# A new order of steps in the first two groups of a fused attention and mixture-of-experts kernel: gated blocks in front of high parts, products in front of low parts and sums, a low part in front of an outer product

## The chip, the cores and the metric
One core of one Trainium2 chip. The metric is the device time of the whole kernel in microseconds (us), the median of several executions; lower is better. The engines are TensorE (PE in the profile: matrix products; PEld is its weight load), VectorE (DVE), ScalarE (ACT), GpSimd (POOL) and SyncE (SP), which here only issues DMAs. Each engine works through its own list of instructions in the order in which they are written; between engines the kernel waits on semaphores that it sets by hand.

## What is computed
The input x is [8, 256, 512]. The first half is a long convolution with outer products of heads, the second a mixture of experts:

```python
def _L0_xattn_ref(v, k, bias, x1, x2, num_heads):       # v = layernorm(x), x1 = x2 = ctx
    vr, x1r, x2r = (t.reshape(B, H, num_heads, L) for t in (v, x1, x2))
    kv = vr[:, :, :, None, :] * x2r[:, :, None, :, :]
    y = irfft(rfft(kv, n=2 * L) * rfft(k, n=2 * L)[None, :, None, None, :])[..., :L]
    y = y + kv * skip
    return jnp.einsum('bhijl,bhil->bhjl', y, x1r).reshape(B, D, L)
...
scores = sigmoid(xf @ gate_w.T)
topk_w, topk_idx = top_k(scores, 2)                      # weights normed to sum 1, times 2.5
shared_out = silu(xf @ shared_wg.T) * (xf @ shared_wu.T) @ shared_wd.T
h = silu(einsum('td,efd->etf', xf, exp_wg)) * einsum('td,efd->etf', xf, exp_wu)
all_out = einsum('etf,edf->etd', h, exp_wd)              # 8 experts, two picked for each token
...
x = x + _L0_xattn_ref(layernorm(x), k, bias, ctx, ctx, 8)
x = x + ffn(layernorm(x))
```

There are 32 head groups (H) of 8 heads, 2048 tokens, 8 experts of width 352, and shared experts of width 704.

## The kernel before, in words
The work has two stages. In the first, the 32 head groups s = 0 to 31 are taken in order, in four groups g of eight (s = 8g + h; HG = 8, G = 4). In the second, 39 tiles of 128 routed rows go through their expert. The shared experts of group g - 1 are computed in between the head groups of group g.

One head group s passes through these steps, and the change and the prediction's steps touch all of them:
- `outer(s)` (L654, instructions of L664, GpSimd): four products of 512 columns, v times context, into one of two buffers kv. It waits for the low part of s - 2, whose buffer it takes over, and outer(8g) also for the turned tiles of group g (L753). `second_outer` is the first one of this kind.
- `high_parts(s)` (L1122, instruction L1126, ScalarE): the half-precision high part of kv, into one of three buffers. It waits for outer(s).
- `low_parts(s)`: what is left of kv. For the s in the list DVE_LOWS (0, 1, 3, 5, 6, 7, 8, 9, 11 and every even s from 14 on) it runs on VectorE as one instruction (L1451, L1454), for the others on GpSimd as four (L687, L692).
- `turn_filter(s)` (L1115, L1119, ScalarE): the filter of s is brought into its form. SP loads the next filter after it (L433).
- `convolve(s)` (L826, TensorE): 30 matrix products of 512 columns through `split_products` (L821 to L823), in four blocks of 3, 6, 9 and 12, each block into its own bank. Block n waits for the low part and for product n of s - 1, which reads the bank that it writes.
- `products(s, h, g, blocks)` (L1462, L1468, VectorE): four products of a bank with the context, and `total(s, h)` (L1473, L1475), the sum over them. `finish` is both.

Between these lie, for a group g: `mix_out` (transposes of the mixed result, L843), which `mixed_tile` (L1648, L1652) reads and adds to x, two banks in turn, so that the third transpose waits for the first mixed tile; `mixed_moments`, the inverse root on GpSimd (L697), `mixed_shift` (L1490), `feed_norm` on ScalarE (L1170) and `feed_low` on VectorE (L1520), after which SP turns the rows (L480) for the gate and the shared experts. A gated block (g, m), m = 0 to 5, is a `gate_up` on TensorE (24 products, 12 for m = 0), which waits for the gated product of block m - 1 (L893); `gated_silu` on ScalarE (L1201), `gated_product` on VectorE (L1624, L1631), `gated_high` on ScalarE (L1208, L1215) and `gated_low` on VectorE (L1634, L1639). The skip term of the attention goes through `skip_product` (L1503, L1510, VectorE), `skip_sum` (L853, L857, TensorE) and `skip_term` (L1513, L1517 and L1518, VectorE); its buffers hm and silu are those of the gated blocks. `values(g)` is a layer norm, `prepare` its transposes and `turned` (L1160, L1166, ScalarE) the copy of these from the banks. `shared(i)` (L1239, L1242 and L1244, ScalarE) and `piece(i)` (L720, L723, GpSimd) split nine pieces of the shared weights into high and low parts. `pick` and `pairs` choose the experts and the rows, and `send_rows` (GpSimd) scatters the rows.

No planner sets the order: each engine's list is written out by hand, in loops over g and h with exceptions, as in ScalarE's list:

```python
for h in range(1, HG + 1):
    ...
    elif 0 < g < G - 1 and h == 6:
        turn_filter(s0 + h + 1)
        turned(g + 1, range(2, Q))
        high_parts(s0 + h + 2)
        gated(g - 1, h - 3)
        continue
```

TensorE's own order (L950 to L1027) and SP's (L488 to L570) are the same before and after.

## Time and profile before

| what | value |
| --- | --- |
| median of 3 runs | 709.83 us (709.59 to 712.0) |
| time of the profiled execution | 713.41 us |
| its span | 711.4 us |
| granted clock of TensorE over the span | 0.976 |
| busy share: TensorE, VectorE, GpSimd, ScalarE | 92%, 63%, 50%, 41% |
| first stage, up to the last convolution of group 3 | to about 398 us |
| first routed tile to the end | from about 478 us |

The span is the time from the first to the last instruction of the profiled execution; its own time is 2.0 us longer, and it is itself 3.6 us longer than the median. A TensorE clock of 1.00 is 2.4 GHz, and 0.5 is 1.2 GHz. Busy shares are means over stages with different limits.

### The profile page before, as it was taken

What the parts mean: (1) busy time and instruction counts of PE and PEld (TensorE: products, weight loads), DVE (VectorE), ACT (ScalarE), POOL (GpSimd) and SP (SyncE); (2) the same over time, 40 slices, a digit from 0 to 9 for tenths busy, and PEclk for the clock granted to TensorE, in tenths of its full rate; (3) what the DMA queues carried; (4) which work ended last, traced back from release to release, by engine and by line L of the source; (5) the groups of instructions that cost most, each with busy time, mean ns of one, the idle gap of its engine ahead of it and who ended that gap; (6) DMA issues with size and microseconds to landing.
All of it is one profiled execution on the core that took longest, in us unless ns stands there. A gap on an engine that the chain in (4) does not pass through costs nothing.

```text
span 711.4 us, 11546 instructions
## 1 busy us (share of the span) xinstructions
PE 655.6 (92%) x3475; PEld 331.4 (47%) x3476; DVE 447.1 (63%) x723; ACT 293.9 (41%) x374; POOL 354.6 (50%) x294
## 2 busy tenths in 40 slices
PE   5979878977999999899999999889979999999994
PEld 3534333433444444344444434345545555555552
DVE  4999988786987695998796778864431221112210
ACT  4356568434233653223541278343432233323321
POOL 2999899925686454695566005600132222332223
PEclk8899999999999999999999999999999999999998
DMA  6944326012234810224313668958998888788864
GB/s 196 289 118 111 98 89 147 17 43 53 102 116 86 182 30 16 90 76 56 94 30 120 249 188 283 384 130 171 237 162 122 126 129 130 129 138 128 132 93 60
DMA packets 130519, 91.57 MB, mean 129 GB/s; under 512 B 96992, under 2 KB 110816, under 8 KB 129952
## 3 DMA queue, kind: packets, MB, share of 16 engines
q1 hardware_dynamic: 121728, 71.49, 41.1%
q0 software_dynamic: 8176, 18.75, 14.5%
q10 hardware_dynamic: 576, 0.82, 0.5%
q8 instruction: 23, 0.38, 0.2%
q14 instruction: 16, 0.13, 0.1%
HBM read 46.32 MB, written 25.65 MB: 101 GB/s over the span
## 4 chain that ended last, share of the span: by engine, by line
PE 55%; DVE 17%; POOL 9%; SPq 5%; ACT 5%; issue 5%; DMA 3%; POOLq 0%; DVEq 0%; ACTq 0%
PE banks L821 16%; PE banks L823 15%; PE banks L822 15%; POOL arena L664 6%; PE banks L913 2%; DVE mixT L1475 2%; DVE arena L1468 2%; PE banks L917 2%; PE banks L918 2%; SPq L583 2%; DVE stats L1481 2%; POOL arena L723 1%; DVE silu L1510 1%; DMA arena<-split_filters 1%; DMA x_tok<-in_x 1%
## 5 line engine op out<-in xcount | busy, mean ns | idle before, releaser
L664 POOL TENSOR_TENSOR arena<-arena 128x512 f32<-128x512 f32 x120 | 141.9, 1214 | 58.7 <-ACT arena L1166 31.5
L783 POOL DMA_INDIRECT out<-xf,ids x39 | 61.7, 1583 | 183.8 <-DMA out<-xf,ids 96.4
L821 PE MATMUL banks<-arena 128*128 128x512 f16 (+1 forms) x330 | 125.0, 379 | 15.8 <-DVE arena L1468 12.1
L822 PE MATMUL banks<-arena 128*128 128x512 f16 (+1 forms) x330 | 124.8, 378 | 0.0
L823 PE MATMUL banks<-arena 128*128 128x512 f16 (+1 forms) x330 | 124.6, 378 | 0.0
L821 PE MATMUL banks<-arena,normed 128*128 x312 | 98.2, 315 | 4.0 <-DVE hm L1853 4.0
L823 PE MATMUL banks<-arena,normed 128*128 x312 | 98.3, 315 | 0.0
L822 PE MATMUL banks<-arena,normed 128*128 x312 | 98.2, 315 | 0.0
L1851 DVE SCALAR_TENSOR_TENSOR hm<-banks,silu 128x256 f32<-128x256 f32 x39 | 16.6, 425 | 121.5 <-PE banks L823 102.5
L1126 ACT ACTIVATE arena<-arena 128x2048 f16<-128x2048 f32 x31 | 59.0, 1904 | 70.6 <-POOL arena L664 68.0
L1468 DVE TENSOR_TENSOR arena<-banks,arena 128x512 f32<-128x512 f32 x128 | 80.5, 681 | 12.2 <-PE banks L823 11.9
L1475 DVE TENSOR_REDUCE mixT<-arena 128x256 f32<-128x2048 f32 x32 | 73.1, 2285 | 1.0
L821 PE MATMUL banks<-xf,arena 128*128 128x512 f16 x176 | 67.0, 380 | 2.6 <-DVE hm L1631 2.6
L692 POOL TENSOR_TENSOR arena<-arena 128x512 f16<-128x512 f32 x56 | 64.0, 1173 | 6.5 <-ACT arena L1126 6.5
L822 PE MATMUL banks<-xf,arena 128*128 128x512 f16 x176 | 66.8, 380 | 0.0
L823 PE MATMUL banks<-xf,arena 128*128 128x512 f16 x176 | 66.7, 379 | 0.0
L821 PEld LDWEIGHTS banks<-arena 128*128 128x128 f16 x330 | 32.7, 99 | 58.2 <-issue 17.3
L1119 ACT ACTIVATE arena<-arena 128x1024 f16<-128x1024 f16 x31 | 32.6, 1052 | 54.0 <-PE banks L823 41.5
L823 PEld LDWEIGHTS banks<-arena 128*128 128x128 f16 x330 | 32.8, 100 | 37.9 <-issue 1.4
L1360 ACT CAST x_tok<-hm 128x384 f16<-128x384 f32 x37 | 18.9, 511 | 73.8 <-DVE hm L1853 71.8
L822 PEld LDWEIGHTS banks<-arena 128*128 128x128 f16 x330 | 32.8, 99 | 35.5 <-issue 1.7
L821 PE MATMUL banks<-arena,mixT 128*128 x117 | 44.4, 379 | 1.2 <-issue 1.2
(196 smaller groups left out, 1082.0 us busy)
## 6 DMA issues: line engine op xcount, KB each, us to landing
arena<-split_filters SPq DMA_DIRECT2D x31, 256.0 KB, 3.7
arena<-in_expert_w SPq DMA_DIRECT2D x12, 544.0 KB, 8.0
stages<-in_expert_w SPq DMA_DIRECT2D x10, 544.0 KB, 4.7
arena<-in_ctx_hidden SPq DMA_DIRECT2D x4, 1024.0 KB, 8.1
arena<-in_ctx SPq DMA_DIRECT2D x8, 512.0 KB, 6.2
out<-x_tok SPq DMA_DIRECT2D x6, 512.0 KB, 5.5
x_tok<-in_expert_w SPq DMA_DIRECT2D x5, 544.0 KB
mixT<-in_expert_w SPq DMA_DIRECT2D x5, 544.0 KB
```

Source lines behind the costliest of these rows:

```text
L664: nc.gpsimd.tensor_tensor(kv[s % 2][:, lb * COLS:(lb + 1) * COLS].rearrange("p (b j i) -> p b j i", i=NH, j=NH), v[:, a, None, :].to_broad ...
L692: nc.gpsimd.tensor_tensor(kvl[s % SPLITS][:, c], kv[s % 2][:, c], kvh[s % SPLITS][:, c], ALU.subtract).then_inc(kvl_by_pool, 1)
L783: nc.gpsimd.indirect_dma_start(out=out, out_offset=bass.IndirectOffsetOnAxis(ap=ids[slot][:, 0:1], axis=0), in_=yg[slot], in_offset=None, ...
L821: nc.tensor.matmul(dst, wh, xh, start=(k == 0), stop=False)
L822: nc.tensor.matmul(dst, wh, xl, start=False, stop=False)
L823: last = nc.tensor.matmul(dst, wl, xh, start=False, stop=(k == n - 1))
L1119: nc.scalar.activation(filt[s % 2].rearrange("p (t l) -> p t l", t=2), backward(filt_raw, 2), ACT.Copy).then_inc(filt_ready, 1)
L1126: nc.scalar.activation(kvh[s % SPLITS], kv[s % 2], ACT.Copy).then_inc(kvh_ready, 1)
L1360: nc.scalar.copy(by_token[slot][:, 0:FK * P], hm[:, 0:FK * P]).then_inc(r_hh, 1)
L1468: nc.vector.tensor_tensor(prod[:, n * COLS:(n + 1) * COLS].rearrange("p (b j i) -> p b j i", i=NH, j=NH), bank[n].rearrange("p (b j i) -> ...
L1475: nc.vector.tensor_reduce(heads(mixT)[:, :, h * NH:(h + 1) * NH], prod.rearrange("p (a j i) -> p a j i", i=NH, j=NH), AX_X, ALU.add).then_ ...
L1851: nc.vector.scalar_tensor_tensor(out=hm[:, 0:whole], in0=up[:, 0:whole], scalar=1 / WS, in1=silu[:, 0:whole], op0=ALU.mult, op1=ALU.mult)
```

## The change
Only orders of steps are changed, on ScalarE, GpSimd and VectorE; `split_products`, the steps themselves and the orders of TensorE and SP are not. By engine:
- GpSimd: in group 1 the low part of h = 7 is issued before the outer product of s = 16 instead of behind it, and shared piece 8 one head group later.
- ScalarE: in group 0 shared piece 3 moves in front of high part 7, so that turned tiles 2 and 3 follow right behind that part; in group 1 shared piece 7 stands in front of filter 11, gated blocks 0, 1, 3 and 5 in front of the high parts beside them; in group 2 the silu and the high copy of gated blocks 2 and 3 are moved in the same way.
- VectorE: in group 0 the moments and low part 3 stand in front of total 1, two or three products in front of low parts 7 and 8; at the start of group 1 three products stand in front of low part 9, total 8 between the third and the fourth mixed tile, and single products and low parts 10 to 12 are interleaved with the feed's low parts; in group 2 the products of s = 19 stand in front of `pick`; in group 3 total 24 stands in front of the fourth mixed tile.

```diff
@@ GpSimd
-            pieces_at = {..., (1, 3): [7], (1, 4): [8]}
+            pieces_at = {..., (1, 3): [7], (1, 5): [8]}
                 for h in range(HG):
-                    low_parts(s0 + h)
+                    if g != 1 or h != HG - 1:
+                        low_parts(s0 + h)
+                    if g == 1 and h == HG - 2:
+                        low_parts(s0 + h + 1)
@@ ScalarE
-            shared_at = {(0, 3): [0], ..., (0, 6): [3], (0, 7): [4], (0, 8): [5], (1, 1): [6], (1, 2): [7, 8]}
+            shared_at = {(0, 3): [0], ..., (0, 7): [4], (0, 8): [5], (1, 1): [6]}
                     if g == 1 and h == 2:
+                        shared(7)
                         next_parts(s0 + h + 1)
+                        shared(8)
+                        load_sigmoid(0)
+                        continue
...
+                    if g == 0 and h == 5:
+                        turned(1, range(0, 2))
+                        turn_filter(h + 1)
+                        shared(3)
+                        high_parts(h + 2)
                         continue
+                    if g == 0 and h == 6:
+                        turned(1, range(2, Q))
+                    elif g == 1 and h == 3:
+                        scores(0)
+                        load_silu(0)
+                        gated(0, 0)
+                        next_parts(s0 + h + 1)
+                        continue
+                    elif g == 1 and h in (4, HG):
                         turn_filter(s0 + h + 1)
+                        gated(0, h - 3)
                         high_parts(s0 + h + 2)
                         continue
+                    elif g == 1 and h == 5:
+                        next_parts(s0 + h + 1)
+                        values(2)
+                        gated(0, 2)
+                        turned(2, range(0, 2))
+                        continue
+                    elif g == 1 and h == 6:
                         turn_filter(s0 + h + 1)
+                        turned(2, range(2, Q))
+                        gated(0, 3)
                         high_parts(s0 + h + 2)
+                        continue
+                    elif g == 2 and h == 5:
+                        turn_filter(s0 + h + 1)
+                        gated_silu(1, 2)
+                        high_parts(s0 + h + 2)
+                        gated_high(1, 2)
+                        turned(3, range(0, 2))
+                        continue
+                    elif g == 2 and h == 6:
+                        turned(3, range(2, Q))
+                        gated_silu(1, 3)
+                        turn_filter(s0 + h + 1)
+                        gated_high(1, 3)
+                        high_parts(s0 + h + 2)
                         continue
@@ VectorE, group 0
             for h in range(1, HG):
-                low_parts(h + 1)
-                finish(h, h, 0)
                 if h == 1:
+                    products(h, h, 0)
                     value_moments(1)
+                    low_parts(3)
+                    total(h, h)
+                    continue
+                if h == 2:
+                    products(h, h, 0)
                     values(1)
+                    total(h, h)
+                elif h >= HG - 2:
+                    products(h, h, 0, range(0, h - HG + 4))
+                    low_parts(h + 1)
+                    products(h, h, 0, range(h - HG + 4, LB))
+                    total(h, h)
+                else:
+                    low_parts(h + 1)
+                    finish(h, h, 0)
@@ VectorE, groups 1 to 3
+                if g == 1:
+                    products(s0, 0, g, range(0, LB - 1))
+                    low_parts(s0 + 1)
+                    products(s0, 0, g, range(LB - 1, LB))
+                    mixed_tile(0, 0)
+                    mixed_tile(0, 1)
+                    mixed_tile(0, 2)
+                    dve.wait_ge(outT_ready, Q * g)
+                    total(s0, 0)
+                    mixed_tile(0, 3)
+                    mixed_moments(0)
+                    mixed_moments(0, True)
+                    products(s0 + 1, 1, g, range(0, 1))
+                elif g == 2:
...
+                else:
+                    low_parts(s0 + 1)
+                    products(s0, 0, g)
+                    mixed_tile(g - 1, 0)
+                    mixed_tile(g - 1, 1)
+                    mixed_moments(g - 1)
+                    mixed_tile(g - 1, 2)
+                    dve.wait_ge(outT_ready, Q * g)
+                    total(s0, 0)
+                    add_shared(g - 2, 0)
+                    mixed_tile(g - 1, 3)
+                    add_shared(g - 2, 1)
+                    mixed_moments(g - 1, True)
                 mixed_shift(g - 1)
                 low_parts(s0 + 2)
...
                 if g == 1:
-                    products(s0 + 1, 1, g)
-                    feed_low(0, range(0, 2))
+                    products(s0 + 1, 1, g, range(1, LB))
+                    feed_low(0, range(0, 1))
                     total(s0 + 1, 1)
-                    feed_low(0, range(2, Q))
+                    feed_low(0, range(1, 3))
+                    products(s0 + 2, 2, g, range(0, 1))
+                    low_parts(s0 + 3)
+                    feed_low(0, range(3, Q))
+                    products(s0 + 2, 2, g, range(1, LB))
+                    total(s0 + 2, 2)
...
                 gated(g - 1, 0)
                 if g == 1:
+                    products(s0 + 3, 3, g, range(LB - 1, LB))
+                    total(s0 + 3, 3)
                     skip_product(1, 0)
                     skip_product(1, 1)
-                    products(s0 + 3, 3, g, range(LB - 1, LB))
-                    total(s0 + 3, 3)
...
+                elif g == 2:
+                    finish(s0 + 3, 3, g)
+                    pick(g - 1)
+                    value_moments(g + 1)
+                    values(g + 1)
+                    gated(g - 1, 1)
```

## Rows read from the trace of the kernel before

**Rows 1.** The page: busy time by engine, and three groups of instructions

```profile
PE 655.6 (92%) x3475; PEld 331.4 (47%) x3476; DVE 447.1 (63%) x723; ACT 293.9 (41%) x374; POOL 354.6 (50%) x294
...
L1468 DVE TENSOR_TENSOR arena<-banks,arena 128x512 f32<-128x512 f32 x128 | 80.5, 681 | 12.2 <-PE banks L823 11.9
L1475 DVE TENSOR_REDUCE mixT<-arena 128x256 f32<-128x2048 f32 x32 | 73.1, 2285 | 1.0
```

**Rows 2.** Windows: stretch, its length, busy by engine, TensorE's clock, DMA share, GB/s

```profile
480.00:700.00 220.00, 214.75 (x1272) 124.92 (x1270) 56.03 (x127) 70.43 (x123) 57.86 (x37) 0.99 0.84 138
```

**Rows 3.** Who TensorE waited for: us in total, times, longest

```profile
PE banks L821 <- DVE arena L1468: 12.1, 7, 3.1
PE banks L857 <- DVE hm L1510: 5.9, 3, 4.5
```

**Rows 4.** Timeline of TensorE: start, us, instruction, count, wait in front and its releaser

```profile
85.97 0.38 PE L821 MATMUL banks<-arena 128*128 128x512 f16 x1 [1.57 <-DVE arena L1468]
96.62 1.70 PE L843 MATMUL banks<-con,mixT 128*128 128x128 f32 x8 [3.15 <-DVE x_tok L1652]
...
116.23 0.38 PE L821 MATMUL banks<-arena 128*128 128x512 f16 x1 [3.06 <-DVE arena L1468]
...
150.14 0.38 PE L821 MATMUL banks<-arena 128*128 128x512 f16 x1 [1.52 <-DVE arena L1468]
160.20 0.39 PE L821 MATMUL banks<-xf,arena 128*128 128x512 f16 x1 [2.56 <-DVE hm L1631]
...
177.99 1.24 PE L857 MATMUL banks<-hm,con 128*128 128x512 f32 x2 [4.49 <-DVE hm L1510]
...
254.42 0.38 PE L821 MATMUL banks<-arena 128*128 128x512 f16 x1 [1.60 <-DVE arena L1468]
...
302.11 1.10 PE L857 MATMUL banks<-hm,con 128*128 128x512 f32 x2 [1.10 <-DVE hm L1510]
```

**Rows 5.** Windows around waits of TensorE; the clock is the third number from the right

```profile
47.00:55.00 8.00, 6.63 (x30) 2.87 (x30) 7.90 (x11) 3.37 (x4) 8.00 (x8) 1.00 0.11 33
...
97.00:101.00 4.00, 4.00 (x16) 2.15 (x15) 3.90 (x7) 3.48 (x3) 4.00 (x4) 0.59 0.65 255
...
116.00:122.00 6.00, 5.77 (x26) 2.38 (x27) 5.45 (x8) 5.49 (x7) 6.00 (x6) 0.72 0.70 176
...
178.00:182.00 4.00, 3.56 (x6) 1.10 (x7) 3.86 (x10) 0.70 (x1) 3.26 (x3) 0.60 0.10 32
```

**Rows 6.** Timeline of VectorE, ScalarE and GpSimd, 65 to 90 us

```profile
67.40 2.58 DVE L1454 TENSOR_TENSOR arena<-arena 128x2048 f16<-128x2048 f32 x1
...
74.62 2.28 DVE L1454 TENSOR_TENSOR arena<-arena 128x2048 f16<-128x2048 f32 x1
...
75.69 1.05 ACT L1166 COPY arena<-banks 128x512 f32<-128x512 f32 x2
...
65.74 6.20 POOL L664 TENSOR_TENSOR arena<-arena 128x512 f32<-128x512 f32 x4
...
76.81 4.14 POOL L664 TENSOR_TENSOR arena<-arena 128x512 f32<-128x512 f32 x4 [2.79 <-ACT arena L1166]
...
83.00 6.22 POOL L664 TENSOR_TENSOR arena<-arena 128x512 f32<-128x512 f32 x4
```

**Rows 7.** Timeline of GpSimd and ScalarE, 97 to 112 us

```profile
104.61 4.50 POOL L692 TENSOR_TENSOR arena<-arena 128x512 f16<-128x512 f32 x4
...
103.70 1.91 ACT L1126 ACTIVATE arena<-arena 128x2048 f16<-128x2048 f32 x1 [1.44 <-POOL arena L664]
```

**Rows 8.** Timeline of ScalarE and VectorE around 172 us

```profile
171.40 1.91 ACT L1126 ACTIVATE arena<-arena 128x2048 f16<-128x2048 f32 x1 [4.24 <-POOL arena L664]
...
173.83 0.69 DVE L1631 SCALAR_TENSOR_TENSOR hm<-banks,silu 128x512 f32<-128x512 f32 x1 [5.39 <-ACT silu L1206]
```

**Rows 9.** Timeline of VectorE and ScalarE in group 2

```profile
253.58 2.48 DVE L1468 TENSOR_TENSOR arena<-banks,arena 128x512 f32<-128x512 f32 x4
...
279.95 1.91 ACT L1126 ACTIVATE arena<-arena 128x2048 f16<-128x2048 f32 x1 [4.25 <-POOL arena L664]
```

37 lines of the change are left out of this document (9 added, 28 removed).

## The prediction
> **What bounds the kernel.** I read five views. The page comes first: TensorE is busy 92% of the span, no other engine over 63% [rows 1]. The windows come second: from 480 us to the end TensorE is busy 214.75 of 220 us at a clock of 0.99 [rows 2], so the routed tiles leave next to nothing, and what comes earlier in time shifts them as a block. Third, who TensorE waits for: 12.1 us for VectorE's products (L1468) in 7 waits and 5.9 us for its skip products (L1510) in 3 [rows 3]. Fourth, where these waits lie: all large ones stand between 84 and 180 us, in the end of group 0 and in group 1, and small ones at 254 and 302 us [rows 4]. Fifth, the clock: behind a wait of 3.06 to 4.49 us it is granted at 0.59 to 0.72 of full (2.4 GHz with stretches of 1.2 GHz), behind the one of 2.93 us in front of 47.6 us it is 1.00 [rows 5]. The three falls cost 41% of 4 us, 28% of 6 us and 40% of 4 us: 1.6 to 1.7 us each, on top of the waits.
>
> I write conv(s), outer(s), high(s), low(s), products(s) and total(s) for the steps of head group s (s = 8g + h), turn(s) for the filter. One conv is 6.5 us, one product 0.62 from start to start, a total 2.2, a low part 2.2 on VectorE and 4.5 on GpSimd, a high part 1.8, four outer products 4.13 when nothing disturbs them [rows 1, 6, 7].
>
> **The change, stage by stage.** No instruction is added or removed; a split products(s) keeps its four instructions. So each term is a start time of TensorE, before and after, worked out along the orders.
>
> *Group 0, h = 1 to 5.* Moments and low(3) go in front of total(1). VectorE has no idle time here and the sum of its work in front of products(2) is the same, so conv(3) and conv(4) keep their starts: 0. GpSimd gets the variance 2.2 us earlier but low(3) now falls in outer(4); I count it 1.3 us earlier, hidden.
>
> *Group 0, h = 6 and 7.* Here the change speaks against itself. Before, low(7) runs at 74.62, while GpSimd is idle: it waits until 76.81 for ScalarE's copy of the turned tiles at 75.69 [rows 6]. After, this copy stands before the shared piece and right behind high(7). That one waits for outer(7), which begins at about 64.5 (65.74 less the 1.3) and has low(6) inside: 64.5 + 4.13 + 2.1 = 70.8, high(7) to 72.7, the copy to 73.6. So outer(8) starts at 73.7, three microseconds earlier; but low(7) now stands behind two products, at 75.86, in the middle of outer(8). What such a meeting costs is shown: outer(9) took 6.22 us with low(8) inside, 2.1 more than alone, and low(6) took 2.58, held up 0.4 us by the outer product that had begun [rows 6]. So low(7) waits for one of outer(8)'s four instructions, 0 to 1.03 us; by the start times above it is 0.9 (next boundary 76.8). It ends at 79.0 and conv(7) starts at 79.1, not 77.75: **1.35 lost**. The same for low(8): in front of it three products, ready at 84.3 (total(6) ends at 82.45), held up until 85.2 by outer(9) (begun at 82.1, behind outer(8) to 80.0 and a shared piece of 2.1), done at 87.4: conv(8) at 87.5, not 85.97 [rows 4]: 1.5 lost in all. The Trainium skill (SBUF — State Buffer, "SBUF: two separate sides") calls the shared port pair of VectorE and GpSimd an exclusive lock that the first to start holds for its whole instruction; the trace agrees, and by this rule these two steps speak against the change.
>
> *Mixed tiles.* conv(8) ends at 94.0. VectorE by then has low(9) (92.5 to 94.8, held behind three products) and one product left, so the first mixed tile is read at 95.45, and TensorE's second pair of transposes starts at 96.25 (before 96.62 [rows 4]). The wait shrinks from 3.15 to 1.3 us because the transposes start later, and the clock should not fall. With total(8) out of the way of the fourth transpose conv(9) starts at 97.3 (98.12) and ends at 103.8, 1.9 us earlier, most of it the clock.
>
> *conv(10) and conv(11).* The moments end at 103.5 behind total(8), so GpSimd's low(10) starts at 104.6, as before [rows 7], and conv(10) at 105.8 waits for its first block, and once more for its second: end 112.8 (113.0). low(11), behind one product of 10, is ready at 112.4, held up 0.8 us by outer(12), done 115.4; turn(11) now stands behind a shared piece and ends at 115.6 (ScalarE's row norm ends at 112.7). conv(11) starts at 115.7 (116.23). So the 3.06 us wait stays, as 2.9 us: it has two causes now. Whether the clock falls behind it the trace does not say: bounds 0 and 1.7 us; nearest is the row of 2.93 us without a fall, so I take 0. End of the first three blocks 119.95 (121.8).
>
> *To conv(13).* Logits, gated block 0, gate_up(0,1), two skip sums: conv(12) starts at 133.4 (135.1). The gated block no longer waits for high(13); product(11,3) is done before the skip products. VectorE goes through skip products, terms, gated(0,1), pick and moments and reaches products(12) at 146.2, where it was at 149.3: conv(13) at 146.9 (150.14 [rows 4]).
>
> *gate_up(0,3).* values(2) end at 153.9, silu 154.4, product 155.15: it starts at 155.2 (160.20), the wait is 1.0 us instead of 2.56. conv(14) at 161.9.
>
> *The large one.* Before, ScalarE does high(16) in front of gated(0,3); high(16) waits until 171.40 for outer(16), VectorE idles 5.39 us for the silu, and TensorE then waits 4.49 us for the skip products behind it [rows 8, 4]. After, gated(0,3) comes at 162.1. VectorE's order decides: products(13) and total(13) end at 163.4, product(0,3) 164.1, copy 164.7, low 165.4, skip products to 168.4, while conv(14) ends at 168.4. Wait gone, and with it 0.43 us for the rank and the fall of the clock (1.6): conv(15) at 175.3, before 187.06, **11.8 earlier**. GpSimd: low(15) now goes into its idle time in front of outer(16) (about 149 to 154), needed at 175; shared piece 8 ends at 149.3, and the copy that waits for it is at 155.2. Queued behind the new waits of ScalarE is high(14), at 136.9 instead of 133.7, needed by VectorE at 156.5. SP: turning the rows comes 3 us later (last low part at 116.0) and filter 12 behind it, landed at about 121, used at 126: hidden. Skip sum (2,2) will wait 0.5 us for gated(0,4). conv(16) at 189.2, before 200.5: **11.3 earlier**.
>
> *Group 2.* products(19) stood behind pick and moments, at 253.58 [rows 9], and cost 1.60 us [rows 4]. After they run first, but pick, moments, inverse root and shift then stand in front of gated(1,1), done at about 260.3 on the old clock, and gate_up(1,2) waits for it: 1.3 of the 1.6 are given back. gated(1,3) no longer waits for high(24), which was released at 279.95 [rows 9]: the waits 0.31, 0.58 and 1.10 in front of the skip sums go. Sum **2.3**.
>
> *Group 3.* Shift 1.6 us later, logits have some 8 us in hand: 0.
>
> **Sum:** 11.3 + 2.3 = 13.6 us. The profiled execution took 713.41 (span 711.4), so 699.8; the median of the three runs shown is 3.58 lower, 709.83, which gives 696.2. I say **696.5**.
>
> **Rivals.** Half a per cent, 3.5 us, is about what a measurement of this kernel can tell from no change.
> *A, the large wait stays* (17%). VectorE reaches gated(0,3) late, or another wait (the rank, the turned tiles) takes its place. For: by my times its skip products end just when conv(14) ends, with no slack. Against: the wait for the silu was 5.39 us. Loss 4.49 + 1.6 of clock, partly: 701.5.
> *B, falls of the clock and held-up low parts in group 1* (10%). conv(10) and conv(11) both wait over 2 us; two falls of 1.7 and two more holds of 1.03 on low(9) and low(11), and a longer wait for mixed tiles, 2 us: 704.
> *C, no change* (4%). The freed time comes back as waits for the experts' weights, whose transfers begin behind group 3. Against: they are all started by events that move with TensorE, and TensorE does not wait there [rows 2]. 709.8.
> *D, slower* (4%): the lock on the port. If ScalarE's copy does not come earlier, low(7) still locks outer(8); GpSimd, which has no idle time from 76.8 to 119 us, is 2.1 us late in every later step, and TensorE's waits for products turn into waits for low parts. With conv(7) 1.35 and conv(8) another 1.5 us late, and nothing won behind them, it ends at 709.8 + 2.1 + 2.9 = 714.8. It decides only when GpSimd is late by more than the slack of low(13), which I find done at 138.1 and used at 146.9, 8.8 us. It is the same rule of the lock; the rule alone, taken as the whole effect, would give this time.
> The forecast keeps 65%.
>
> **Range.** With no hold of low(7) and low(8) the chain reaches conv(16) 13.6 instead of 11.3 us earlier (-2.3), and if group 2 gives back nothing, -1.3; to the small waits behind 404 us I leave 2: 690.5 at the low end. Upward the clock (+1.7), the holds, A and B: 704.5. Outside lie C, D and a part of B, with some doubt in so long a chain. Below 706.3 (faster by over 0.5%) lie the forecast, A and nearly all of B: 91%; within 0.5%: 5%; slower: 4%.
>
> **What would show it.** Right: no wait of TensorE near 175 us before the first skip sum of group 2 and VectorE's silu wait of 5.39 us gone; conv(16) about 11 us earlier; low(7) longer than 2.3 us or outer(8) about 6.2 us; conv(7) later than 77.75; a wait of about 2.9 us still in front of conv(11); a new wait below 1.3 us in front of gate_up(1,2). Wrong: any wait over 2 us between 120 and 190 us; a clock below 0.9 behind conv(11); a routed stage that takes more than before from its first tile to its end.

## The result, and the profile of the changed kernel

| | before | after |
| --- | --- | --- |
| median | 711.33 us (709.05 to 714.25, 12 runs) | 705.5 us (701.37 to 709.77, 12 runs) |
| profiled execution, its span | 713.41 us, 711.4 us | 709.77 us, 707.7 us |
| granted clock over the span | 0.976 | 0.974 |
| conv(8), conv(16), conv(31), each after the start of conv(1) | 57.17, 171.72, 362.33 | 61.61, 168.28, 358.56 |
| from conv(31) to the end of the span | 320.3 | 320.3 |

The ratio of after to before is 0.9924, 95% interval 0.9895 to 0.9952: faster by 5.8 us, where I had forecast 13.6, and outside my range. The direction was right, the size was not. A few executions of low15_undone, of h6_low15 and of before beside them were far slower at a lower clock (770 to 1332 us); every median, number of runs and ratio below is of the others. Starts in the tables are read in the timeline of TensorE and counted from conv(1) of the same execution; the rows shown have the time from the start of the span.

The page of after, its busy times and the groups that answer to [rows 1] (VectorE's products are now L1500, its totals L1507, its low parts L1486; TensorE's lines are three higher):

```profile
PE 656.8 (93%) x3475; PEld 332.2 (47%) x3476; DVE 454.9 (64%) x723; ACT 294.3 (42%) x374; POOL 346.2 (49%) x294
...
L1500 DVE TENSOR_TENSOR arena<-banks,arena 128x512 f32<-128x512 f32 x128 | 80.7, 680 | 10.6 <-PE banks L826 10.2
L1486 DVE TENSOR_TENSOR arena<-arena 128x2048 f16<-128x2048 f32 x17 | 46.4, 2728 | 0.0
```

The low parts in before (groups by line):

```profile
L1454 DVE TENSOR_TENSOR arena<-arena 128x2048 f16<-128x2048 f32 x17 | 40.5, 2382 | 2.6 <-ACT arena L1126 2.6
```

VectorE has the same 723 instructions and is busy 7.8 us more. The products cost what they did; the 17 low parts cost 5.9 us more, with a mean of 2.73 us instead of 2.38, and a low part that nothing disturbs takes 2.28 [rows 6]. That is the first place to look.

The timeline of TensorE in after, the rows with a wait (start, us, instruction, wait in front and its releaser), against [rows 4]:

```profile
48.59 0.38 PE L824 MATMUL banks<-arena 128*128 128x512 f16 x1 [3.85 <-DVE arena L1500]
...
82.03 0.38 PE L824 MATMUL banks<-arena 128*128 128x512 f16 x1 [1.65 <-issue]
90.48 0.38 PE L824 MATMUL banks<-arena 128*128 128x512 f16 x1 [1.82 <-issue]
...
100.25 1.85 PE L846 MATMUL banks<-con,mixT 128*128 128x128 f32 x8 [2.25 <-DVE x_tok L1684]
...
120.00 0.39 PE L824 MATMUL banks<-arena 128*128 128x512 f16 x1 [2.48 <-ACT arena L1122]
...
137.96 1.10 PE L860 MATMUL banks<-hm,con 128*128 128x512 f32 x2 [0.65 <-DVE hm L1542]
139.53 1.10 PE L860 MATMUL banks<-silu,con 128*128 128x512 f32 x2 [0.47 <-DVE silu L1542]
161.76 0.39 PE L824 MATMUL banks<-xf,arena 128*128 128x512 f16 x1 [0.42 <-DVE hm L1663]
...
190.18 1.10 PE L860 MATMUL banks<-hm,con 128*128 128x512 f32 x2 [1.65 <-DVE hm L1542]
...
258.18 0.39 PE L824 MATMUL banks<-xf,arena 128*128 128x512 f16 x1 [2.04 <-DVE hm L1663]
...
298.40 1.10 PE L860 MATMUL banks<-hm,con 128*128 128x512 f32 x2 [1.50 <-DVE hm L1542]
```

The wait of 4.49 us near 178 is gone, as forecast. What was not forecast: waits all through group 0, and 2.04 and 1.50 us in group 2. Windows around the new waits (the clock is the third number from the right):

```profile
101.00:105.00 4.00, 4.00 (x17) 2.09 (x16) 3.56 (x4) 1.85 (x1) 2.12 (x3) 0.65 0.24 54
...
120.00:124.00 4.00, 4.00 (x12) 1.57 (x13) 3.93 (x5) 3.97 (x4) 4.00 (x3) 0.61 0.65 144
```

So two of the three falls of [rows 5] are still there, behind waits of 2.25 and 2.48 us, shorter than the 2.93 us in front of 47.6 behind which before had a clock of 1.00. I had taken all three as gone. One is there that before did not have: behind the 3.85 us in front of 48.6 the stretch from 47 to 55 us has 0.79, where before had 1.00 [rows 5].

Which of these waits has a fall behind it is not fixed by the kernel. low15_undone (below) has the same orders as after up to this point and the same wait in front of conv(11), and its clock stays at 1.00 (a row of the timeline and a window):

```profile
119.38 0.39 PE L821 MATMUL banks<-arena 128*128 128x512 f16 x1 [2.48 <-ACT arena L1119]
120.00:124.00 4.00, 4.00 (x45) 2.17 (x44) 3.93 (x5) 3.98 (x4) 4.00 (x4) 1.00 0.81 200
```

And gates_only (below) has before's orders in group 0 and the same wait of 2.93 us in front of conv(3), and its clock falls, where before's did not:

```profile
47.73 0.38 PE L824 MATMUL banks<-arena 128*128 128x512 f16 x1 [2.93 <-DVE arena L1496]
47.00:55.00 8.00, 7.28 (x26) 3.00 (x27) 7.90 (x11) 3.37 (x4) 8.00 (x8) 0.79 0.11 33
```

The same holds of two more waits: 2.25 us at the mixed tiles (0.57 over 100 to 104 us in after, 1.00 in h6_undone) and 2.54 us in front of conv(10) (1.00 over 105 to 109 us in moments_first, 0.62 in moments_g2v); in each pair the kernels have the same orders up to there. So each profile holds falls that another execution of the same kernel may not have.

The starts, counted from conv(1), and the stretch in which the change lies, for all kernels of this study:

| kernel | conv(8) | conv(12) | conv(15) | conv(16) | conv(31) | conv(8) to (16) | conv(31) to end |
| --- | --- | --- | --- | --- | --- | --- | --- |
| before | 57.17 | 106.28 | 158.26 | 171.72 | 362.33 | 114.55 | 320.3 |
| after | 61.61 | 111.59 | 153.02 | 168.28 | 358.56 | 106.67 | 320.3 |
| g0_only | 61.62 | 106.64 | 160.95 | 174.32 | 365.09 | 112.70 | 315.5 |
| g0_undone | 57.14 | 104.09 | 148.18 | 163.44 | 354.59 | 106.30 | 319.2 |
| h1_undone | 57.78 | 104.26 | 148.34 | 163.60 | 354.26 | 105.82 | 314.4 |
| moments_first | 57.91 | 106.54 | 148.00 | 163.26 | 353.39 | 105.35 | 316.3 |
| piece_split | 57.66 | 104.75 | 148.92 | 164.18 | 355.99 | 106.52 | 314.8 |
| h6_only | 57.17 | 104.61 | 153.22 | 171.47 | 362.98 | 114.30 | 316.9 |
| gates_only | 57.15 | 107.03 | 148.46 | 163.72 | 355.54 | 106.57 | 320.0 |
| h6_undone | 61.62 | 110.95 | 157.66 | 171.03 | 360.91 | 109.41 | 317.7 |
| low15_undone | 61.63 | 108.08 | 153.68 | 171.94 | 360.62 | 110.31 | 320.2 |
| h6_low15 | 57.15 | 106.28 | 153.22 | 168.47 | 358.80 | 111.32 | 316.2 |
| start_undone | 58.10 | 105.60 | 148.66 | 163.92 | 353.47 | 105.82 | 316.7 |
| g2_undone | 61.63 | 111.52 | 152.98 | 168.23 | 359.47 | 106.60 | 317.3 |
| h1_g2v_undone | 57.74 | 104.20 | 148.28 | 163.53 | 353.93 | 105.79 | 319.2 |
| moments_g2v | 57.91 | 103.50 | 147.57 | 162.82 | 353.00 | 104.91 | 317.4 |
| split_best | 58.09 | 106.14 | 150.30 | 165.56 | 354.94 | 107.47 | 317.0 |

The last column scatters by 6 us between kernels that differ in nothing there (more on it at the end). The column conv(31) is the finer instrument, and the medians stand beside it. How fine it is shows in kernels that are the same up to some point: moments_first and moments_g2v, the same up to conv(16), are 3.04 us apart at conv(12), where the clock fell behind conv(11)'s wait in one and not in the other, and still 0.44 at conv(16); after and low15_undone, the same up to there, are 3.51 apart at conv(12). From conv(16) to conv(31) the six kernels with after's order of group 2 and uncut pieces take between 188.7 and 191.2 us. A difference of 1 us at conv(31), or of 3 at conv(12), is not a finding by itself.

### The profile page after: what moved, and what is told of

The parts are those of the page before. It is cut to its first block, busy times and chain, and to the rows that moved or that the text cites. A ratio compares the mean times of both kernels' runs of the same rounds, so it can differ in the third digit from the quotient of the medians.

```text
span 707.7 us, 11553 instructions
## 1 busy us (share of the span) xinstructions
PE 656.8 (93%) x3475; PEld 332.2 (47%) x3476; DVE 454.9 (64%) x723; ACT 294.3 (42%) x374; POOL 346.2 (49%) x294
## 4 chain that ended last, share of the span: by engine, by line
PE 53%; DVE 26%; issue 6%; SPq 5%; ACT 5%; DMA 3%; POOLq 0%; POOL 0%; DVEq 0%; ACTq 0%
PE banks L824 15%; PE banks L825 15%; PE banks L826 15%; DVE arena L1500 5%; DVE mixT L1507 4%; DVE arena L1486 3%; PE banks L916 2%; DVE stats L1513 2%; PE banks L921 2%; PE banks L920 2%; SPq L583 1%; DVE silu L1542 1%; PE banks L846 1%; DMA arena<-split_filters 1%; DVE hm L1663 1%
## 5 line engine op out<-in xcount | busy, mean ns | idle before, releaser
L664 POOL TENSOR_TENSOR arena<-arena 128x512 f32<-128x512 f32 x120 | 134.0, 1148 | 51.3 <-DVE arena L1486 31.6
L1500 DVE TENSOR_TENSOR arena<-banks,arena 128x512 f32<-128x512 f32 x128 | 80.7, 680 | 10.6 <-PE banks L826 10.2
L1507 DVE TENSOR_REDUCE mixT<-arena 128x256 f32<-128x2048 f32 x32 | 73.1, 2284 | 1.1 <-PE banks L846 0.2
L692 POOL TENSOR_TENSOR arena<-arena 128x512 f16<-128x512 f32 x56 | 65.8, 1203 | 6.5 <-ACT arena L1129 6.5
L1486 DVE TENSOR_TENSOR arena<-arena 128x2048 f16<-128x2048 f32 x17 | 46.4, 2728 | 0.0
```

The source lines that it names most:

```text
L664: nc.gpsimd.tensor_tensor(kv[s % 2][:, lb * COLS:(lb + 1) * COLS].rearrange("p (b j i) -> p b j i", i=NH, j=NH), v[:, a, None, :].to_broad ...
L692: nc.gpsimd.tensor_tensor(kvl[s % SPLITS][:, c], kv[s % 2][:, c], kvh[s % SPLITS][:, c], ALU.subtract).then_inc(kvl_by_pool, 1)
L1486: nc.vector.tensor_tensor(kvl[s % SPLITS], kv[s % 2], kvh[s % SPLITS], ALU.subtract).then_inc(kvl_by_dve, 1)
L1500: nc.vector.tensor_tensor(prod[:, n * COLS:(n + 1) * COLS].rearrange("p (b j i) -> p b j i", i=NH, j=NH), bank[n].rearrange("p (b j i) -> ...
L1507: nc.vector.tensor_reduce(heads(mixT)[:, :, h * NH:(h + 1) * NH], prod.rearrange("p (a j i) -> p a j i", i=NH, j=NH), AX_X, ALU.add).then_ ...
```

## Experiments on group 0

**g0_only**: the kernel before with the change's orders of group 0 alone.

```
             for h in range(1, HG):
-                low_parts(h + 1)
-                finish(h, h, 0)
...
+                if h == 1:
+                    products(h, h, 0)
+                    value_moments(1)
+                    low_parts(3)
+                    total(h, h)
+                    continue
...
```

> The kernel before with the new order of group 0 alone. Theory H: conv(8) starts at about 90.5 instead of 86, and the kernel is 3 to 4.5 us slower than before, about 715. Theory L: as before, 711.

Measured 711.64 us (12 runs), ratio 1.0001 (0.998 to 1.0022). conv(8) at 61.62, exactly after's 61.61 (before 57.17): group 0 alone loses 4.45 us there, and conv(31) comes 2.8 us later than in before. The median doesn't show it: it is 711.64, where before's own runs beside it had 711.44, as theory L had it and not theory H. The table shows where the 4.45 us go. At conv(12) 0.36 us of them is left: the wait in front of the mixed tiles is 0.93 us instead of 3.15 and no fall is behind it (1.00 over 97 to 101 us, before 0.59). The rest of the 2.8 us at conv(31) begins behind the wait of 2.56 us in front of gate_up(0,3), which before has too, but here with a fall of the clock (0.59 over 160 to 164 us, before 1.00). So in the kernel before, with its own long waits in group 1, the loss of group 0 is absorbed nearly whole.

**g0_undone**: the opposite, the kernel after with group 0 as before, on VectorE and on ScalarE.

```
-                        turn_filter(h + 1)
-                        shared(3)
-                        high_parts(h + 2)
+                        next_parts(h + 1)
...
+                low_parts(h + 1)
+                finish(h, h, 0)
...
```

> The changed kernel with all of group 0 put back to the old order (VectorE's head groups 1, 2, 6, 7 and ScalarE's shared piece 3). Theory H (VectorE's low parts are held up by GpSimd instructions that the new order of group 0 puts in front of them): conv(8) starts at 86, not 90.5, low parts 5 to 9 take 2.3 to 3.2 us each as before, and the whole is 4 to 5 us faster than the changed kernel, about 701. Theory L (group 0 costs nothing of note, the missing gain was never there in groups 1 and 2): within 1 us of the changed kernel, about 705.5.

Measured 701.95 us (6 runs), ratio 0.9867 (0.9827 to 0.9906); conv(8) 57.14, conv(31) 354.59, 4.0 us better than after. In the kernel after the loss of group 0 goes through to the end nearly whole; from conv(8) to conv(16) the two take 106.67 and 106.30 us. Why it is not absorbed here as in g0_only was not tried.

**h1_undone** and **moments_first** take the step of h = 1 apart. The first has total(1) in front of both the moments and low(3), as before; the second leaves the moments where the change put them and moves low(3) alone.

```
                 if h == 1:
-                    products(h, h, 0)
+                    finish(h, h, 0)
                     value_moments(1)
                     low_parts(3)
-                    total(h, h)
                     continue
```

```
                     value_moments(1)
-                    low_parts(3)
                     total(h, h)
+                    low_parts(3)
                     continue
```

> The changed kernel with only the step at h = 1 put back (total 1 in front of the moments and low part 3). Theory H in the form that this step starts it (GpSimd gets 1.3 us ahead, so that its shared pieces of 2.1 us stand in front of low parts 5 and 6): low(3) takes 2.3 instead of 3.2 us, low(5) and low(6) together 6 instead of 8.1 us, conv(6) starts at 71 instead of 73.7, and the kernel is 2 to 3 us faster than the changed one, about 703. If the later steps (products in front of low parts 7 and 8) are the cause: less than 1 us.

> The changed kernel with low part 3 behind total 1 again, but the moments still in front of both: of the step at h = 1 only the moments stay moved. If the moved low part (a hold of 1 us, and GpSimd released 1.3 us early) starts the loss: as with the whole step put back, low(3) 2.3 us, low(5) 3.2 us, conv(31) begins 353 to 354.5 us behind conv(1) instead of 358.6. If the early variance (the moments) is what puts GpSimd out of step: conv(31) stays at about 358.6 behind conv(1).

h1_undone 703.57 us (6 runs), ratio 0.9888 (0.9859 to 0.9918), conv(8) 57.78; moments_first 701.87 us (4 runs), ratio 0.9859 (0.9805 to 0.9913), conv(8) 57.91. Of the 4.44 us at conv(8) they get back 3.83 and 3.70. So it is not the moments, and the steps of h = 6 and 7, against which my prediction argued at length, are worth the remaining 0.6 to 0.7 us at most and not 1.5 (low(7), which I had held up, takes 2.28 us in h1_undone): it is low(3) in front of total(1). The timelines show how. The low parts on VectorE and GpSimd's instructions in after:

```profile
42.32 3.20 DVE L1486 TENSOR_TENSOR arena<-arena 128x2048 f16<-128x2048 f32 x1
60.27 4.27 DVE L1486 TENSOR_TENSOR arena<-arena 128x2048 f16<-128x2048 f32 x1
69.17 3.83 DVE L1486 TENSOR_TENSOR arena<-arena 128x2048 f16<-128x2048 f32 x1
...
60.26 2.13 POOL L723 TENSOR_TENSOR arena<-xf,arena 128x1024 f16<-128x1024 f32 x1
64.62 4.14 POOL L664 TENSOR_TENSOR arena<-arena 128x512 f32<-128x512 f32 x4 [2.23 <-DVE arena L1486]
68.71 2.13 POOL L723 TENSOR_TENSOR arena<-arena 128x1024 f16<-128x1024 f32 x1
```

and the same in moments_first:

```profile
59.83 3.20 DVE L1486 TENSOR_TENSOR arena<-arena 128x2048 f16<-128x2048 f32 x1
67.66 2.59 DVE L1486 TENSOR_TENSOR arena<-arena 128x2048 f16<-128x2048 f32 x1
...
56.75 4.14 POOL L664 TENSOR_TENSOR arena<-arena 128x512 f32<-128x512 f32 x4
60.85 4.18 POOL L723 TENSOR_TENSOR arena<-xf,arena 128x1024 f16<-128x1024 f32 x1
64.99 6.19 POOL L664 TENSOR_TENSOR arena<-arena 128x512 f32<-128x512 f32 x4
```

In after, GpSimd begins a shared piece, one instruction of 2.13 us, at 60.26; VectorE's low part begins at 60.27, ends at 64.54 and so takes 4.27 us instead of 2.28: it stood for the whole piece. GpSimd's next outer product then waits 2.23 us, until the low part is done, so that it comes behind it again, and so does the next piece. That order feeds itself: low parts 5 to 9 took 4.27, 3.83, 2.98, 3.10 and 3.73 us. It begins with low(3), which takes 3.20 us in front of total(1) and 2.28 behind it: counted from conv(1), low(5) starts at 31.40 instead of before's 30.76, and GpSimd's outer(5) at 17.50 instead of 18.90. This is not scatter: in g0_only, g2_undone, h6_undone and low15_undone, which have the same order of group 0, low parts 5 to 8 take the same within 0.01 us. In moments_first VectorE's low part falls into the outer products, whose single instructions are about 1.03 us, and takes 3.20 and 2.59; there it is GpSimd that stands (4.18 and 6.19 us instead of 2.13 and 4.14), and GpSimd had time. The Trainium skill (SBUF — State Buffer, "SBUF: two separate sides") has the port pair locked by the one that starts first, for a whole instruction; these rows agree for low parts, outer products and pieces: whoever comes second pays what is left of the other's instruction. Not every instruction of VectorE meets GpSimd: the 32 totals (L1507) take 2.27 to 2.29 us each in after, with GpSimd busy beside them or not.

**piece_split** tests this by the length of the instruction: the order of after, unchanged, with each shared piece cut in four on GpSimd.

```
-                nc.gpsimd.tensor_tensor(shared_piece(i, d_l, gu_l), as_piece(shared_raw(i), i),
-                                        shared_piece(i, d_h, gu_h), ALU.subtract).then_inc(shared_l, 1)
+                whole = (shared_piece(i, d_l, gu_l), as_piece(shared_raw(i), i), shared_piece(i, d_h, gu_h))
+                for k in range(4):
...
```

> The changed kernel with each shared piece on GpSimd as four instructions of a quarter each. Theory H: a low part waits for at most one of these, 0.55 us, in place of up to 2.1; low parts 5 to 9 take 2.2 to 2.9 us each, conv(8) starts 2 to 4 us earlier than at 90.5, the whole about 702 to 703. Rival (the low parts wait for GpSimd's whole run of work, not for one instruction, or GpSimd paces the chain): the low parts stay at 3 to 4.3 us and the time within 1 us of 705.5, or above it for the 27 added instructions.

Measured 702.75 us (6 runs), ratio 0.9882 (0.9846 to 0.9918), conv(8) 57.66. low(3) still takes 3.21 us, but low parts 5 to 9 take 2.81, 2.38, 2.28, 2.29 and 2.70, and of the 4.44 us of group 0 0.49 is left although every order is after's. Two doubts can be settled from the trace. The cut makes GpSimd 0.45 us late before low(5), which could have let low(5) go first; but it still begins 0.01 us behind GpSimd, at 60.88 behind 60.87, and takes 0.53 us more than alone, a quarter of 2.13. And the clock, which fell behind conv(3)'s wait in after, did not fall here (1.00 over 49 to 53 us); but VectorE begins products(3) 26.44 us behind conv(1) here and 26.42 in after, so that fall moved nothing on VectorE. With this the cause is shown from both sides: by the order and by the length of the instruction that stands in the way.

## Experiments on group 1

**h6_only** is the step of the large wait, alone on the kernel before. The prediction's 11.8 us at conv(15) are the sum of all steps up to there; 6.8 of them are this step's, from conv(14) to conv(15).

```
                         turned(g + 1, range(2, Q))
+                        if g == 1:
+                            gated(g - 1, h - 3)
                         high_parts(s0 + h + 2)
-                        gated(g - 1, h - 3)
+                        if g == 2:
+                            gated(g - 1, h - 3)
```

> The kernel before with one step moved: gated block (0, 3) in front of high part 16 on ScalarE. Theory G (this step is what the large gain in group 1 comes from): the wait of 4.49 us in front of the first skip sum of group 2 goes with its fall of the clock, conv(15) begins 5 to 6.7 us earlier, the kernel 5 us faster, 706. Rival (the gain needs VectorE to be ahead from the start of group 1): VectorE reaches the skip products late, the wait shrinks by under 2 us, 709.5.

Measured 711.0 us (10 runs), ratio 0.999 (0.9959 to 1.0021). conv(15) comes 5.0 us earlier, and conv(16) 0.25: all but nothing is left. The wait for the silu is gone and another one stands behind it. Theory G was right for conv(15) and wrong for the time, where it had 706.

**gates_only** is the kernel before with all moves of the gated blocks in group 1, with low(15) and piece 8 on GpSimd, product(11,3) on VectorE and the small step of group 3, and nothing in group 0, at the start of group 1 or in group 2.

```
+                    elif g == 1 and h == 3:
+                        scores(0)
+                        load_silu(0)
+                        gated(0, 0)
+                        next_parts(s0 + h + 1)
+                        continue
+                    elif g == 1 and h in (4, HG):
...
```

> The kernel before with one part of the change: in group 1 the gated blocks stand in front of the high parts on ScalarE (h = 3, 4, 5, 6 and 8), low(15) in front of outer(16) on GpSimd and product(11,3) with total(11) in front of the skip products. Group 0, the start of group 1 and group 2 are as before. Theory (VectorE paces group 1, and what the change wins is its idle time in front of the silu): conv(8) to conv(16) takes 114.55 us before and 106.67 after; of the 7.9 us the stretch from conv(12) on has 8.7 and the stretch up to it -0.9, so the gated blocks alone give all of it. conv(16) minus conv(1) 171.72 before, here 162.5 to 164.5, VectorE's idle time for the silu between conv(8) and conv(16) 3 to 5 us instead of 12.5, conv(31) minus conv(1) 353.5 to 355.5 (before 362.33), median 701 to 704. Rival (my prediction's steps: the start of group 1 carries part of it, because it decides when VectorE reaches the gated blocks): the gates alone give only 5 to 6 us, conv(31) minus conv(1) 356.5 to 357.5. Second rival (what gated(0,3) alone showed: what is won in one place is given back at the next, so without group 0's earlier turned tiles nothing is won): within 1 us of before, 361.5 to 363.

Measured 701.77 us (5 runs), ratio 0.9838 (0.9792 to 0.9883): the part is faster than the whole. conv(8) to conv(16) 106.57 us (before 114.55, after 106.67), VectorE's idle time for the silu there 4.5 us instead of 12.5. conv(31) at 355.54 is at the upper edge of the theory's interval. The gates with low(15) hold the whole gain of group 1.

**h6_undone** is after with gated(0,3) behind high(16) again.

```
                         turned(2, range(2, Q))
-                        gated(0, 3)
                         high_parts(s0 + h + 2)
+                        gated(0, 3)
                         continue
```

> The kernel after with gated(0,3) behind high(16) again, everything else of the change kept: the step to which my prediction gave 11.8 us. Theory (VectorE paces group 1; gated(0,3) in front of high(16) is what keeps VectorE from the idle time for the silu; alone it won nothing only because VectorE's later gated blocks waited): VectorE idles 3 to 6 us longer for the silu, TensorE waits over 3 us in front of skip_sum(2,0) again, conv(15) 4 to 6 us later than after's 153.02 behind conv(1), conv(16) 3 to 6 us later than 168.28 behind conv(1), conv(31) minus conv(1) 361.5 to 364.5, median 708 to 711. Rival (the same 0 here as when the step was made alone): conv(16) within 1 us, conv(31) minus conv(1) 358 to 359.5. Rival of my prediction's sum (the whole large wait with its fall of the clock): 11 us lost, conv(31) minus conv(1) 368 to 370.

Measured 707.57 us (11 runs), ratio 0.9932 (0.9902 to 0.9962). TensorE waits 3.44 us in front of skip_sum(2,0), VectorE idles 5.39 us for the silu, conv(15) is 4.6 us later than after's and conv(16) 2.75, conv(31) 2.35 (a little less than the theory had). The rival with 11 us had taken the prediction's sum up to conv(15) for the step. The step is worth 0 alone and 2.4 to 2.75 in company, so something in the company belongs to it. The timeline of VectorE in h6_only, a part of the sixteen instructions between rank and products(14), shows what:

```profile
177.28 1.03 DVE L1567 TENSOR_TENSOR wsum<-top 128x4 f32<-128x4 f32 x1
178.35 0.99 DVE L1571 TENSOR_SCALAR wsum<-wsum 128x4 f32<-128x4 f32 x1
...
180.40 0.99 DVE L1575 TENSOR_SCALAR stages<-wtop 128x4 f32<-128x4 f32 x1
```

the same instructions in gates_only:

```profile
174.00 0.15 DVE L1592 TENSOR_TENSOR wsum<-top 128x4 f32<-128x4 f32 x1
174.19 0.17 DVE L1596 TENSOR_SCALAR wsum<-wsum 128x4 f32<-128x4 f32 x1
...
174.81 0.17 DVE L1600 TENSOR_SCALAR stages<-wtop 128x4 f32<-128x4 f32 x1
```

and GpSimd, in h6_only:

```profile
171.74 5.39 POOL L692 TENSOR_TENSOR arena<-arena 128x512 f16<-128x512 f32 x4
177.22 4.15 POOL L664 TENSOR_TENSOR arena<-arena 128x512 f32<-128x512 f32 x4
```

Three instructions of four numbers a row take 1 us each where they took 0.15 to 0.17, and one of eight numbers 0.77 where it took 0.17: each stands behind one of GpSimd's instructions of 1.03 us. The other twelve of the sixteen hardly change. From the rank to the next products VectorE needs 7.83 us here, 3.88 in before (whose pairs begin 5 us later; GpSimd is through at 181.26, and only the first of them meet it) and 4.43 in gates_only and after, where low(15), L692, has been done long before, and GpSimd's last outer product ends just before wsum, the first row shown, begins: at 173.86 in gates_only (wsum at 174.00), at 178.38 in after (178.52). The gain of the early silu was paid back in these tiny instructions: 5.39 us of idle time less 3.95 more for the pairs. The next two kernels test this reading.

**low15_undone**: after with only GpSimd's low(15) back in its old place. **h6_low15**: before with h6_only's move and that of low(15).

```
-                    if g != 1 or h != HG - 1:
-                        low_parts(s0 + h)
-                    if g == 1 and h == HG - 2:
-                        low_parts(s0 + h + 1)
+                    low_parts(s0 + h)
```

> The kernel after with low(15) back in its old place on GpSimd, behind outer(16). Theory (in gated(0,3) alone, what the early silu won on VectorE, 5.39 us of idle time, was given back by the sixteen tiny instructions of the rank and the pairs: from the first of them to products of conv(15) they took 7.83 us where the kernel before took 3.88 and the gates alone 4.43, because each stood behind one instruction of about 1 us of low(15) or an outer product on GpSimd; the move of low(15) empties GpSimd in that stretch): here this stretch on VectorE takes 7 to 8 us instead of after's 4.43, conv(16) comes 2.5 to 5 us later than after's 168.28 behind conv(1), conv(31) minus conv(1) 361 to 363.5 (after 358.56), median 708 to 710.5. Rival (my prediction's view: low(15) only fills idle time of GpSimd, needed at 175, so its place is worth nothing): conv(16) within 0.5 us, conv(31) minus conv(1) 358 to 359.

> The kernel before with two moves: gated(0,3) in front of high(16) on ScalarE, and low(15) in front of outer(16) on GpSimd. gated(0,3) alone won nothing (conv(16) minus conv(1) 171.47, before 171.72). Theory (the two belong together: low(15) out of the way keeps the tiny instructions of the pairs short, and then VectorE reaches the skip products of group 2 in time): VectorE's stretch from the rank to the products of conv(15) 4 to 4.9 us instead of 7.83, the wait in front of skip_sum(2,2) under 1.5 us instead of 2.96 and no fall of the clock behind it, conv(16) minus conv(1) 165.5 to 168, conv(31) minus conv(1) 356.5 to 359, median 704.5 to 708. Rival (the pairs are not the cause: the other gated blocks that stand behind high parts, at h = 4 and 5, make VectorE late): conv(16) minus conv(1) over 169.5, conv(31) minus conv(1) 360 to 363.

low15_undone 710.56 us (8 runs), ratio 0.9989 (0.9957 to 1.002): without this one move, which I had put down as filling idle time, the time cannot be told from before's. The pairs take 7.83 us again and conv(16) comes 3.66 us later than after's, 3.0 of it between conv(15) and conv(16), where h6_only and h6_low15 differ by the same 3.0. Part of that comes back in group 2: conv(31) is 2.1 us later, less than the theory's 2.4 to 4.9, and still 1.7 us earlier than before's. The other 3 us of the median are not in the first stage. h6_low15 704.92 us (5 runs), ratio 0.9913 (0.988 to 0.9946): the pairs take 4.42 us, the wait in front of skip_sum(2,2) is 1.65 us instead of 2.96, and conv(16) is at 168.47 instead of 171.47 (the theory's interval ended at 168; this execution had a fall behind gate_up(0,3) that h6_only's had not, and its conv(14) is 2.2 us later than there). Row by row TensorE in h6_only and, behind it, in h6_low15:

```profile
192.08 1.10 PE L857 MATMUL banks<-hm,con 128*128 128x512 f32 x2 [2.96 <-DVE hm L1513]
193.01 1.62 PE L857 MATMUL banks<-silu,con 128*128 128x512 f32 x2
```

```profile
189.43 1.10 PE L860 MATMUL banks<-hm,con 128*128 128x512 f32 x2 [1.65 <-DVE hm L1516]
190.37 1.02 PE L860 MATMUL banks<-silu,con 128*128 128x512 f32 x2
```

The second row of each pair shows the clock as well: the same two products take 1.62 us behind the wait of 2.96 and 1.02 behind that of 1.65. h6 and low(15) are one step in two places. Together they are worth 3.25 of the 8.0 us at conv(16), in an execution with one fall more than before's; the other gated blocks are the rest.

**start_undone** is h1_g2v_undone (below) with the start of group 1 put back on VectorE: mixed tiles, moments, low parts for the logits.

```
                 if g == 1:
-                    products(s0, 0, g, range(0, LB - 1))
                     low_parts(s0 + 1)
-                    products(s0, 0, g, range(LB - 1, LB))
-                    mixed_tile(0, 0)
...
+                    products(s0, 0, g)
+                    mixed(g - 1)
...
```

> The kernel after with h = 1 of group 0 and VectorE's step of group 2 as before (the fastest so far), and with VectorE's order at the start of group 1 (mixed tiles, moments, copies of the logits' low parts, products(9) and (10)) put back too. Theory (VectorE's work at the start of group 1 counts as soon as group 0 is not late): conv(8) to conv(12) took 49.11 us before and 46.46 in the fastest, so here about 49 again; what VectorE then has in idle time for the silu (3.6 us between conv(8) and conv(16)) shrinks and takes back 1 to 2 of the 2.6: conv(16) minus conv(8) 106.5 to 108 (fastest 105.79), conv(31) minus conv(1) 354.5 to 356, median 702 to 704. Rival (the start of group 1 wins nothing, its new waits of 0.4 to 0.9 us are all it does): conv(8) to conv(12) 46 to 47, conv(31) minus conv(1) 353 to 354.

Measured 702.03 us (5 runs), ratio 0.9839 (0.9787 to 0.9891). conv(8) to conv(12) takes 47.50 us, 1.04 more than in h1_g2v_undone, and conv(8) to conv(16) 105.82 against 105.79: nothing. What the start of group 1 wins up to conv(12) is lost again by conv(16). VectorE's idle time for the silu, 3.65 us against 3.43, accounts for 0.2 us of it; the rest was not traced. The rival was right, though for conv(12) neither number was.

## Experiments on group 2, and the two mends together

**g2_undone** puts group 2 back on VectorE and ScalarE. **h1_g2v_undone** puts back VectorE's step of group 2 and the step of h = 1. **moments_g2v** is moments_first with VectorE's step of group 2 put back. VectorE's part of the edit is the same in all three:

```
-                    finish(s0 + 3, 3, g)
                     pick(g - 1)
                     value_moments(g + 1)
+                    finish(s0 + 3, 3, g)
                     values(g + 1)
                     gated(g - 1, 1)
```

> The changed kernel with group 2 in the old order on ScalarE and VectorE. As forecast (the new order of group 2 wins 2.3 us): conv(25) begins 2.3 us later, counted from conv(17), the kernel about 2 us slower than the changed one, 707.5. By the trace of the changed kernel (waits of 2.04 and 1.50 us in place of 1.60, 0.31, 0.58 and 1.10): no more than 0.3 us between the two.

> The changed kernel with the step at h = 1 put back and the products of s = 19 behind pick and moments again (VectorE in group 2 as before, ScalarE as after). If the wait of 2.05 us in front of gate_up(1,2) comes from pick, moments and shift standing behind the products: it falls below 0.3 us, the 1.6 us in front of conv(20) come back, net 0.4 us, and the skip sums of group 3 no longer wait 1.5 us: conv(25) begins 1 to 2 us earlier than in the run with h = 1 alone put back, about 702. If the skip sum's wait has another cause: equal to that run within 0.5 us.

> The kernel after with two mends: in group 0 the moments in front of total(1) but low(3) behind it (moments_first gave the shortest first stage, 353.39), and VectorE's step of group 2 as before. Theory (the hold of the low parts begins with low(3), and the step of group 2 is worth 0.3 us): low parts 5 to 9 at 2.2 to 2.9 us, TensorE's wait at gate_up(1,2) 0.4 instead of 2.04 us and 1.8 at conv(20) instead, conv(31) minus conv(1) 352.8 to 353.8, median 700 to 702.5. Rival (the two don't add up: later moments in group 2 shift the wait to the skip sums): 353.9 to 355.

g2_undone 706.16 us (10 runs), ratio 0.9913 (0.9883 to 0.9943): conv(31) 359.47 against after's 358.56, the median within the scatter of after's. That is neither the 2.3 us of the forecast nor the at most 0.3 of the other theory. From conv(16) to conv(31) the six kernels with before's order of group 2 take 190.3 to 191.8 us and the six with after's and uncut pieces 188.7 to 191.2: the step is worth between nothing and 1 us. The waits of before are back, TensorE in g2_undone:

```profile
243.43 0.39 PE L824 MATMUL banks<-xf,arena 128*128 128x512 f16 x1 [0.29 <-DVE hm L1661]
250.58 0.38 PE L824 MATMUL banks<-arena 128*128 128x512 f16 x1 [1.79 <-DVE arena L1498]
...
282.69 1.10 PE L860 MATMUL banks<-hm,con 128*128 128x512 f32 x2 [0.30 <-DVE hm L1540]
284.37 1.13 PE L860 MATMUL banks<-silu,con 128*128 128x512 f32 x2 [0.58 <-DVE next_row L1585]
298.24 1.10 PE L860 MATMUL banks<-hm,con 128*128 128x512 f32 x2 [1.10 <-DVE hm L1540]
```

These sum to 4.06 us, those of after (2.04 and 1.50) to 3.54. h1_g2v_undone 701.54 us (6 runs), ratio 0.9842 (0.9797 to 0.9888), conv(31) 353.93 against h1_undone's 354.26: 0.3 better; its skip sum in front of 293.6 still waits 1.50 us, which that expectation had wrong, so the wait does not come from VectorE's part of group 2; that it comes from ScalarE's is what is left, no run has that part alone. moments_g2v 701.05 us (4 runs, 700.07 to 701.3), ratio 0.9853 (0.9826 to 0.988): conv(31) at 353.0 is the shortest first stage of all, 5.6 us better than after. It does not show that the two mends add up: the 0.39 us to moments_first at conv(31) are there at conv(16) already, where both kernels are the same. VectorE's part is worth 0.3 us in one pair and nothing in the other.

**split_best** is h1_g2v_undone with the shared pieces cut in four as well.

> The kernel after with h = 1 of group 0 and VectorE's step of group 2 as before, and the shared pieces' low parts on GpSimd split in four instructions each: the two mends of what the change lost, together. Theory (both remove the same hold, the low part on VectorE behind one GpSimd instruction of 2.1 us): they do not add up. Low parts 5 to 9 at 2.2 to 2.7 us, conv(8) minus conv(1) 56.8 to 57.8, conv(31) minus conv(1) 353 to 354.5, median 700.5 to 702.5 (fastest so far 701.54). Rival (they add up, because later holds in group 1, low(9) and low(11) and the skip products, go too): conv(31) minus conv(1) 351 to 352.5, median 699 to 700. Rival (27 more GpSimd instructions make GpSimd late in group 1): conv(9) to conv(12) over 37.5 us, median 703 or more.

Measured 702.68 us (5 runs), ratio 0.9852 (0.9805 to 0.9899). The mends of group 0 do not add up, as the theory had it, but conv(8) at 58.09 and conv(31) at 354.94 miss its intervals, and conv(31) is 1.0 us worse than without the cut. The start of group 1 is later: the wait in front of the mixed tiles is 2.33 us instead of 0.97 in h1_g2v_undone, conv(9) comes 1.7 us later, and conv(10) waits 3.84 us instead of 3.40 for GpSimd's low part:

```profile
108.11 0.38 PE L828 MATMUL banks<-arena 128*128 128x512 f16 x1 [3.84 <-POOL arena L692]
```

A piece in four takes 2.56 us instead of 2.13, and conv(10) comes 2.2 us later than without the cut. Where no low part stands behind the piece, the cut only costs.

## Why the prediction was wrong, step by step

Differences of starts, in us, plus is a gain over before:

| stretch | forecast | after |
| --- | --- | --- |
| conv(1) to conv(8) | -1.5 | -4.4 |
| conv(8) to conv(9) | +2.3 | +0.8 |
| conv(9) to conv(11) | -0.3 | 0.0 |
| conv(11) to conv(12) | +1.2 | -1.6 |
| conv(12) to conv(14) | +3.3 | +3.8 |
| conv(14) to conv(15) | +6.8 | +6.7 |
| conv(15) to conv(16) | -0.5 | -1.8 |
| conv(16) to conv(31) | +2.3 | +0.3 |

- **Failed: "VectorE has no idle time here and the sum of its work in front of products(2) is the same ... 0", and the 1.3 us earlier GpSimd "hidden".** The sum of the work is the same only while no instruction meets another. low(3) itself met outer(4) and took 3.20 us instead of 2.28: conv(3) starts 0.92 us later than before's and conv(4) 1.41. Then low(5) came 0.6 us later and GpSimd 1.4 earlier, and that put every shared piece in front of a low part. I priced the meeting for low(7) and low(8), by outer products at most 1.03 us, and forgot that a piece is one instruction of 2.13. Measured 4.4 us lost instead of 1.5. Rival D named this mechanism, but only from h = 6 on and as a loss to GpSimd; the losing engine was VectorE.
- **Failed: "bounds 0 and 1.7 us; nearest is the row of 2.93 us without a fall, so I take 0"** for conv(11), and "the clock should not fall" behind the mixed tiles. Both fell, the second behind 2.48 us. The row of 2.93 was one execution, and with the same wait the clock fell in gates_only; the same 2.48 us had no fall in low15_undone. So neither 0 nor 1.7 could be chosen from a row; the chance of each belonged into the sum. Two new waits for skip products, 0.65 and 0.47, make the rest of the -1.6; with after's orders there they appear only where the clock fell. Without a fall conv(11) to conv(12) takes 17.39 in h1_undone and 17.42 in low15_undone, near my 17.7. The step at the mixed tiles holds in h1_undone, where the wait is 0.98 us and conv(8) to conv(9) takes 9.49, near my 9.8; but there conv(10) waits 3.41 us, with a fall behind it (0.58 over 105 to 109 us), and conv(9) to conv(10) takes 10.04 where I had 8.5.
- **Right in size, wrong in its reason: the large one.** conv(14) to conv(15) 6.7 against 6.8. But I gave it to gated(0,3) alone and took low(15) as filling idle time. The runs show that it takes both: gated(0,3) alone and the change without the move of low(15) are both within 0.2% of before.
- **Mis-sized: what comes behind it.** Skip sum (2,2) waits 1.65 us, not 0.5, with the pairs at 4.43 us instead of before's 3.88, and this in every kernel that has the gates and the move of low(15): VectorE paces group 1. Its idle time for the silu between conv(8) and conv(16) went from 12.5 to 4.5 us, and that 8.0 is near the 7.9 that the stretch became shorter. The two need not agree: h6_low15 has 5.4 us less of idle time and a stretch 3.2 shorter, low15_undone 8.9 less and 4.2 shorter, with the pairs 4.0 longer. h1_undone, moments_first, start_undone and h1_g2v_undone, with quite different starts of group 1, all take 105.4 to 105.8 us for it. So the gains that I added up in front of conv(12) were not to be had twice.
- **Mis-sized: group 2.** I had 1.3 of 1.6 us given back at gate_up(1,2); it was more than all (2.04 for 1.60), and 1.50 us at the skip sum where I had the waits gone. 2.3 forecast, 0.3 measured against before and 0.9 against g2_undone.
- **Right:** the wait at 178 and the 5.39 us are gone; the routed tiles move as a block (320.3 and 320.3 us; that the two agree so well is luck, by the scatter of that column). One of my signs of being wrong came, a clock below 0.9 behind conv(11) (0.61), and it is one that another execution need not show. Rival B, two falls of the clock and held-up low parts, is what happened, one stage earlier and larger, at 705.5 instead of 704; I gave it 10%.

In the two profiled executions the stretches add up to the 3.8 us: group 0 -4.4, group 1 +7.9, nearly all of it the gates with low(15) and nothing that can be told the start of group 1, group 2 +0.3. As separate changes they do not: group 0 costs 4.0 us in after and, but for the clock, next to nothing in before, so that gates_only, with 6.8 us at conv(31), beats the whole change. The medians differ by 5.8, 2 us more; that is within what the stretch behind conv(31) scatters by, in which both profiled executions were long (after's is also the slowest of its twelve).

## What to carry to other kernels

When an order on VectorE or GpSimd changes, list which single instruction of one will be running when one of the other begins: where the two meet, the price is what is left of that instruction, be the waiting one 2048 columns wide or four. The trace tells which instructions meet: compare the durations of one shape. Keep chains of tiny instructions where GpSimd is idle, and count the order that an earlier start brings about, since a meeting can repeat itself in every round. Where one engine paces a stretch, add up its idle time and not TensorE's waits, and take off what its instructions become longer. And before a difference of 2 or 3 us between two traces is given to a step, look whether the clock fell in one of them behind a wait that both have.

## What was not expected of the hardware

- Two meetings of the same low part differ by which GpSimd instruction is in progress: 4.27 us behind one of 2.13, 3.20 behind one of about 1.03, 2.28 alone. In a chain of sixteen tiny instructions four went from 0.15 to 0.17 us to 0.77 to 1.03, and the chain from 4.43 to 7.83 us (3.88 in before).
- The granted clock fell behind waits of 2.25, 2.48, 2.54 and 2.93 us in one execution and not in another, with the same orders up to there and the same wait. Neither the length nor the place alone decides, and what does stays open. One fall costs 1.6 to 1.7 us of TensorE at once, and with the new waits that stand only behind it the stretch from conv(11) to conv(12) is 3.0 us longer (20.46 us in after, 17.42 in low15_undone).
- From conv(31) to the end took 314.4 to 320.3 us in seventeen kernels that do the same there. The profiled executions differ where the last experts' weights arrive. ScalarE in before and in after waits 4 us for them:

```profile
526.11 1.11 ACT L1230 ACTIVATE arena<-mixT 128x1088 f16<-128x1088 f32 x1 [4.12 <-DMA mixT<-in_expert_w]
```

```profile
520.87 1.11 ACT L1233 ACTIVATE arena<-mixT 128x1088 f16<-128x1088 f32 x1 [4.35 <-DMA mixT<-in_expert_w]
```

  The silu of the routed tiles comes every 5.52 us, but in before once after 10.6, in after after 10.8 and then 6.4 and 6.7, in h1_undone after 7.8; over 505 to 545 us the clock is 0.96, 0.91 and 1.00 in the three. Why the weights are later in one execution than in another was not tried and stays open; it makes 5 us of scatter, as much as the whole change.
